# Liquid-scan block of a two-layer kernel: scan products per sequence, four array quadrants, stacked sums, full-row biases and a new order of all engines

## What is computed

```python
x = x + liquid_scan_block(attention_1(x))     # L0_cond, then L0_attn
x = x + experts(attention_2(x))               # L0_cond2, then L0_ffn

# the scan block, 512 channels d, 16 states n, one sequence at a time
xn = rmsnorm(x); x_in, z = split(xn @ in_proj_w); x_in = silu(x_in)
a_mod = sigmoid(x_in @ A_proj_w + A_proj_b)
B, C  = x_in @ B_proj_w, x_in @ C_proj_w
h_t = a_t[:, None] * sigmoid(A_base) * h_{t-1} + B_t[None, :] * x_t[:, None]
y_t = h_t @ C_t
out = x + ((y + D * x_in) * silu(z)) @ out_proj_w
```

## Time and profile before

| | us |
|---|---|
| median of 3 runs (lowest, highest) | 1818.32 (1817.47, 1819.48) |
| the profiled execution | 1821.07 |
| its span, first to last instruction | 1819.1 |
| PE busy in the span | 1633.8 (90%) |
| DVE, ACT, POOL busy | 1153.7 (63%), 915.6 (50%), 857.0 (47%) |
| one iteration in the steady stretch | 51.5 |

### The profile page before, as it was taken

One profiled execution on the slowest core, in us unless ns is written; L12 is line 12 of the kernel. 1 busy time (PEld: TensorE's weight loads), 2 busy tenths in 40 slices (PEclk: granted clock), 3 DMA queues, 4 the chain that ended last, 5 costly groups with the idle time before them and its releaser, 6 DMA issues.

```text
span 1819.1 us, 32943 instructions
## 1 busy us (share of the span) xinstructions
PE 1633.8 (90%) x11663; PEld 1264.5 (70%) x11663; DVE 1153.7 (63%) x2536; ACT 915.6 (50%) x2231; POOL 857.0 (47%) x552
## 2 busy tenths in 40 slices
PE   2248999999999999999999999999999999999875
PEld 1136777777777777777777777777777777777653
DVE  2465666677667666676676666776676666766533
ACT  0224555555555555565555555555555555655421
POOL 1024555554444555554445555544445555545431
PEclk9579999999999999999999999999999999999987
DMA  7110000000000000000000000000000000000000
GB/s 223 53 30 7 2 10 10 10 1 11 10 10 10 10 10 10 4 8 11 10 10 10 10 10 10 1 10 10 11 10 10 10 10 4 8 10 7 7 4 6
DMA packets 40357, 28.19 MB, mean 15 GB/s; under 512 B 19826, under 2 KB 38274, under 8 KB 40196
## 3 DMA queue, kind: packets, MB, share of 16 engines
q1 hardware_dynamic: 40196, 26.09, 5.5%
HBM read 21.37 MB, written 4.71 MB: 14 GB/s over the span
## 4 chain that ended last, share of the span: by engine, by line
PE 71%; ACT 10%; DVE 10%; issue 6%; SPq 2%; POOL 1%; DMA 0%; POOLq 0%; DVEq 0%; ACTq 0%
PE bank L736 13%; PE bank L674 13%; PE bank L702 7%; PE bank L813 6%; PE bank L628 5%; PE bank L630 5%; PE bank L629 5%; ACT a_prob L989 5%; PE bank L828 3%; PE bank L715 3%; PE bank L658 2%; DVE a_sum L1258 2%; DVE a_xn L1185 2%; PE bank L728 2%; SPq L454 2%
## 5 line engine op out<-in xcount | busy, mean ns | idle before, releaser
L1598 POOL TENSOR_TENSOR resid<-xres,a_c 128x256 f32<-128x256 f32 x32 | 23.2, 726 | 337.8 <-DVE x L1359 337.7
L1618 POOL TENSOR_TENSOR y<-y,u 128x512 f32<-128x512 f32 x128 | 162.9, 1272 | 39.1 <-DVE u L1351 34.0
L1610 POOL TENSOR_TENSOR u<-xe,Ef 128x512 f32<-128x512 f32 x96 | 130.2, 1370 | 35.1 <-ACT Ef L1086 35.1
L674 PEld LDWEIGHTS bank<-a_xnT,a_wq 128*128 128x128 f32 x1024 | 125.3, 193 | 17.2 <-issue 14.1
L813 PE MATMUL bank<-u,Gm 128*128 128x512 f32 x256 | 130.7, 614 | 4.5 <-DVE Gm L1343 3.8
L628 PE MATMUL bank<-w_e_hi,cT_hi 128*128 128x512 f32 x256 | 120.8, 472 | 10.2 <-DVE c_c L1407 10.2
L736 PEld LDWEIGHTS bank<-a_wo,a_prob 128*128 128x128 f32 x512 | 95.7, 192 | 48.9 <-ACT a_prob L989 36.9
L736 PE MATMUL bank<-a_wo,a_prob 128*128 128x256 f32 x512 | 119.6, 387 | 10.5 <-ACT a_prob L989 10.5
L674 PE MATMUL bank<-a_xnT,a_wq 128*128 128x128 f32 x1024 | 126.0, 277 | 0.0
L1579 POOL TENSOR_TENSOR a_prob<-a_prob,a_mask 128x1024 f32<-128x1024 f32 x32 | 75.6, 2361 | 104.9 <-DVE a_prob L1229 104.9
L674 PE MATMUL bank<-c_xnT,c_wq 128*128 128x128 f32 x1024 | 124.5, 280 | 0.0
(11 more groups left out here) (290 smaller groups left out, 4406.8 us busy)
## 6 DMA issues: line engine op xcount, KB each, us to landing
a_xin<-in_x SPq DMA_DIRECT2D x32, 128.0 KB, 2.6
xres<-in_x SPq DMA_DIRECT2D x32, 128.0 KB, 2.7
out<-acc SPq DMA_DIRECT2D x32, 128.0 KB, 1.7
a_wq<-in_L_cond_Wq SPq DMA_DIRECT2D x1, 1024.0 KB, 5.0
a_wo<-in_L_cond_Wo SPq DMA_DIRECT2D x1, 1024.0 KB, 6.3
c_wq<-in_L_cond_Wq SPq DMA_DIRECT2D x1, 1024.0 KB
c_wo<-in_L_cond_Wout SPq DMA_DIRECT2D x1, 1024.0 KB
u<-in_L_ffn_expert_w SPq DMA_DIRECT2D x3, 256.0 KB, 4.7
```

The costliest lines, as they stand in the source:

```text
L674: mm = pe.matmul(bank(f"q{half}")[:, m * P:(m + 1) * P], X.wq[:, k, hp * P:(hp + 1) * P], X.xnT[:, k, :], start=k == 0, stop=k == KD - 1)
L1610: pool.tensor_tensor(u[l][:, :], xi[:, :], (E0u if l == 0 else Ef[l])[:, :], ALU.mult)\
L1618: pool.tensor_tensor(y[:, :], y[:, :], tm[l][:, :], ALU.add).then_inc(g.done(f"y{l}"), 1)
```

## The change

Nothing of the result changes; the scan's pair products are confined to one sequence, where the mask had zeros before.

- **G** becomes two float32 matmuls, one for each sequence, of a 128 x 64 operand with 256 columns; `Gm`, the mask and the signs `sums` have 64 instead of 128 columns for each level.
- **mix** becomes two steps, `m0` (levels 0 and 1) and `m1` (levels 2 and 3). Each issues four products of 64 x 64 with 512 columns. The even level ("s", straight) writes each sequence to its own half of bank `m0s`, the odd level ("x", crossed) writes each sequence to the other half of bank `m0x`. So both row halves write into one bank. For the odd levels DVE's product with `Ef` is two instructions of 64 partitions.
- **E**: for each sequence `nl_stacked[b]` holds the high part in its own 64 partitions and the low part in the other 64. One fp32r matmul with the signs of two levels side by side (128 x 128) gives both levels of one sequence: 4 matmuls instead of 8. ACT then takes `exp` per level and sequence, 10 instructions of 64 partitions instead of 5 of 128; the high part takes two `Ln` of 64 partitions and a wait behind them, DVE's low part two instructions.
- **Biases**: decay bias, expert bias and their all-ones or one-hot operands get 128 rows (zeros elsewhere).
- **Order and banks**: `ORDER` and `TURNS` are written anew. Among others `a.W` (output projection of the first attention) and its statistics go from lag 1 to 2, so for tile 0 behind the second setup; SP issues the position-bias transfers one iteration earlier, ahead of iteration 3's loads.

```diff
-    pe.matmul(banks["b.G"][:, :], BTt[:, :], CD[:, :, :], start=True, stop=True)
+    for b in range(BT):
+        seq = slice(b * S, (b + 1) * S)
+        mm = pe.matmul(banks["b.G"][seq, 0:NLV * S], BTt[:, seq], CD[:, :, seq], start=True, stop=True)
...
-    for n, part in enumerate(nl_parts):
-        mm = pe.matmul(banks[f"b.E{l}"][:, :], sums[:, l * P:(l + 1) * P], part[:, :], start=n == 0, stop=n == 1)
+    pe.matmul(banks[f"b.E{n}"][:, :], sums[:, pair * P:(pair + 1) * P], nl_stacked[b][:, :], start=True, stop=True)
...
-    pe.wait_ge(*pool.at(f"u{l}", t))
-    pe.matmul(banks[f"b.m{l}"][:, :], Gm[:, l, :], u[l][:, :], start=True, stop=True)
+    for unit, l in (("s", straight), ("x", crossed)):
+        for b in range(BT):
+            seq, side = slice(b * S, (b + 1) * S), b if unit == "s" else 1 - b
+            mm = pe.matmul(banks[f"b.m{pair}{unit}"][side * S:(side + 1) * S, :],
+                           Gm[seq, l, :], u[l][seq, :], start=True, stop=True)
...
+    for i in range(2):
+        l = 2 * pair + i
+        src = banks[f"b.E{n}"][i * S:(i + 1) * S, :]
+        if l == 0:
+            act.activation(E0u[seq, :], src, ACT.Exp).then_inc(a.done(f"E0u{b}"), 1)
...
+        act.activation(Ef[l][seq, :], src, ACT.Exp, scale=-1.0).then_inc(a.done(f"E{l}{b}"), 1)
...
-    a_bias_parts = sb("decay_bias", [33, 2, D + NST], F32R)
+    a_bias_parts = sb("decay_bias", [P, 2, D + NST], F32R)
...
-    b_e_parts = sb("b_e_parts", [LVW + NE, D], F32R)
+    b_e_parts = sb("b_e_parts", [P, D], F32R)
...
 TURNS = {
+    2: """
+        b.E3@3>act.E31 b.m0s@3>dve.t0 b.xt@2>dve.yl b.x@2>dve.xi c.xt@3>act.xnT c.S1@3>dve.S1""",
...
+    6: """
+        c.ex3@5>dve.ac7 b.m1x@3>dve.t3 b.z@2>dve.zi b.E0@2>act.E10""",
+    7: """
+        b.E1@3>act.E11 b.m0x@3>dve.t1 c.W@4>dve.cn c.q0@3>act.q0 c.S0@3>dve.S0 c.oT@4>act.oT b.G@2>dve.Gm""",
```

More of the change, by code:

```diff
@@ L90, in constants @@
     parts["neg_count_c"] = -np.stack(count_c, 1)
-    parts["scan_mask"] = np.concatenate(masks, 1)
+    parts["scan_mask"] = np.concatenate([np.tile(a[0:S, 0:S], (2, 1)) for a in masks], 1)
     parts["level_rows"] = (tok[:, None] // LVW == np.arange(NLV)[None, :]) * 1.0
@@ L95, in constants @@
     parts["distance"] = (S - 1 - tok)[:, None]
-    parts["sums"] = np.concatenate(sums, 1)
+    stacked = [np.tile(a[0:S, 0:S], (2, 1)) for a in sums]
+    parts["sums"] = np.concatenate(stacked, 1)
     at, n = {}, 0
@@ L107 @@
     "pe": """
[L108 to L111, removed]
+        b.E1@3 c.ex2@5 b.E3@3 a.W@2 c.ex3@5 b.m0@3 c.eb@5 a.xt@1 c.PT0@4 c.PT1@4 a.kv@1 c.O@4 b.m1@3 a.q0@1
@@ L119 @@
[L119 to L122, removed]
+        b.BC@3 c.qs@4 c.ac1@5 a.mk@1 b.ag@3 c.S0@4 c.S1@4 b.nh@3 a.st@0 b.zi@3 b.Gm@3 c.ac2@5 c.mx@4 c.sub@4
+        c.ac3@5 c.ac4@5 c.den@4 a.st2@2 c.ac5@5 c.ac6@5 a.c@2 c.ac7@5 c.out@5 b.t0@3 b.t1@3 b.xn@2 b.t2@3
@@ L123 @@
+        b.t3@3 a.K@1 a.V@1 b.yl@2 c.st2@4 c.c@4 a.xn@0 c.cl@4 a.S0@1 b.xg@2 c.lg@4 c.oh@4 c.ac0@4 c.mk@3
+        b.xi@2 b.x1@3 c.st@3 c.xn@3 a.S1@1 c.ks@3 b.xl@2 a.mx@1 c.V@3 a.sub@1 c.K@3 b.zg@2 a.den@1""",
     "pool": """
[L124 to L125 removed]
+        a.norm@2 c.addb@4 c.addm@4 b.dx@3 b.u0@3 b.u1@3 c.norm@4 b.u2@3 b.u3@3 b.y0@3 b.y1@3 b.y2@3 b.y3@3
+        b.y@3 a.addm@1 c.qsq@3 b.resid@2""",
@@ L126 @@
     "sp": """
[L127 removed]
+        a.mask@1 b.xres@3 a.x@0 c.mask@3 c.store@5""",
 }
@@ L370, in build @@
         nl = yT[:, :, :].rearrange("p k n -> p (k n)")
-        nl_parts = parts("nl", [P, E2])
+        nl_stacked = [sb(f"nl_seq{b}", [P, E2], F32R) for b in range(BT)]
         ae = nl
@@ new lines, in G, with E @@
+                    mm.then_inc(p.done("G"), 1)
+                def E(n):
+                    pair, b = n // BT, n % BT
+                    def run(t):
+                        pe.wait_ge(*banks.free(f"b.E{n}", t))
+                        if n == 0:
+                            pe.wait_ge(*dve.at("nl1", t))
+                        pe.matmul(banks[f"b.E{n}"][:, :], sums[:, pair * P:(pair + 1) * P], nl_stacked[b][:, :],
+                                  start=True, stop=True).then_inc(p.done(f"E{n}"), 1)
@@ L833, in scan @@
                         "G": G, "yT": yT_, "out": out_} | {f"E{l}": E(l) for l in range(NLV)}\
-                    | {f"m{l}": mix(l) for l in range(NLV)}
+                    | {f"m{n}": mix(n) for n in range(NLV // 2)}
             def experts():
@@ L1063, in log_a @@
                     act.wait_ge(*p.at("E3", t - 1))
-                    act.activation(nl_parts[0][:, :], ae[:, :], ACT.Ln).then_inc(a.done("nh"), 1)
+                    for b in range(BT):
+                        seq = slice(b * S, (b + 1) * S)
+                        act.activation(nl_stacked[b][seq, :], ae[seq, :], ACT.Ln).then_inc(a.done(f"nh{b}"), 1)
+                    act.wait_ge(*a.at("nh1", t))
                     act.activation(nl[:, :], ae[:, :], ACT.Ln).then_inc(a.done("nl"), 1)
@@ L1113, in oT @@
                     act.wait_ge(*p.at("eb", t - 1))
-                    act.copy(ohT[:, :], banks["c.oT"][0:LVW + NE, 0:P]).then_inc(a.done("oT"), 1)
+                    act.copy(ohT[:, :], banks["c.oT"][:, 0:P]).then_inc(a.done("oT"), 1)
                 return {"cT": cT_, "le": le_, "oT": oT}
@@ L1328, in nh @@
                     dve.wait_ge(*p.at("E3", t - 1))
-                    dve.tensor_tensor(nl_parts[1][:, :], nl[:, :], nl_parts[0][:, :].bitcast(F32), ALU.subtract)\
-                       .then_inc(d.done("nl"), 1)
+                    for b in range(BT):
+                        seq, other = slice(b * S, (b + 1) * S), slice((1 - b) * S, (2 - b) * S)
+                        dve.tensor_tensor(nl_stacked[b][other, :], nl[seq, :], nl_stacked[b][seq, :].bitcast(F32),
+                                          ALU.subtract).then_inc(d.done(f"nl{b}"), 1)
                 def BC(t):
```

128 lines of the change are left out of this document (63 added, 65 removed), and 5 rows, old and new, of the table RESULTS.

## The result

The changed kernel takes 1857.0 us (median of 4 runs, 1848.0 to 1862.5) beside 1818.9 for the kernel before on the same chip: the ratio is 1.0197, its 95% interval 1.0146 to 1.0247. It is slower by about 2%, and 142 us above the forecast of 1715. The profiled execution took 1854.69 us, its span 1852.9; 30 intervals of an iteration make up nearly all of it, so I read one iteration first, from one E0 to the next. Columns as in the earlier trace rows: busy us and instructions of PE, PE's weight loads, DVE, ACT and POOL, then the clock.

What follows compares the result with a forecast made beforehand. PE was taken as the bound: 46.5 us of work plus a 1.9 wait gave a 48.4 us iteration, 3.1 shorter. 30 x 3.1 + 7 + 3 = 103 us saved gave 1715 us, range 1665 to 1788.

Steps and rivals of the forecast that it cites:

- PE's work, 46.5 an iteration: PE's busy time per iteration falls from 49.94 to 46.5 us through mixes, G, E and biases, less a loss for order.
- Rivals 1 and 2: In new mixes, row halves take turns at a bank (about 1788, 0.10), or quadrants do not overlap (about 1854, 0.05).
- the expert bias: On PE, the expert-bias product falls from 0.31 to about 0.12 us as a full product; gain 0.39 with its successor.
- The half instructions: DVE's two instructions for the low part of `nl`, taken at 0.7 to 1.43 us each.
- the first path: From c's last score product through ACT's exponentials, `prob`, `den` and `norm` to c.PT0: about 15.0 us.
- the second: From `nl` through DVE's low-part halves, statistics and `zi` to E0, then PE's work up to c.PT0: 13.2 to 14.7 us.
- The stall of 1.9 ahead of c.PT0: PE waits 1.9 us per iteration for the softmax's `norm` ahead of c.PT0, or in parts at earlier waits.
- The query-norm wait of 1.3 goes.: PE's 1.3 us wait for the second attention's query norms disappears, because a score step now stands between `qs` and `qt`.
- Rival 3: Longer softmax path, from slower ACT halves and DVE's contention with POOL or a late bank: 1748 to 1781 us, chance 0.18.
- The clock: PE ran at full clock (2.4 GHz, granted 1.00) before; the forecast has no term for a lower one.
- The ends, 7 + 3: Outside the steady iterations: 7 us gained at the start by an earlier second setup, 3 us in the draining.

Runs made afterwards that it cites:

- nl in PSUM: Changed kernel in the same order, but ACT writes the exact logarithm to a free PSUM bank, so DVE's low-part halves read PSUM and SBUF: 1769.0 us, ratio 0.9691 to before.

## Why the prediction was wrong, step by step

- *PE's work, 46.5 an iteration.* Right: 46.3 in the changed kernel, 46.49 with nl in PSUM. Rivals 1 and 2 (row halves in turn, no overlap) are out: a group of mixes costs what PV costs. Only the expert bias missed its price, 0.32 for 0.12, behind the small form.
- *The half instructions, "0.7 to 1.43 each".* This is the step that failed. They took 2.42 each. The upper end was read from the earlier trace rows as a price, and it was a price beside one particular neighbour, POOL's y product of 1.31 us. POOL's row of the kernel before shows it:

```profile
949.55 1.31 POOL L1603 TENSOR_TENSOR y<-xe,d_row 128x512 f32<-128x512 f32 x1
```

  POOL ends at 950.86, the low part at 951.40, 0.54 later. In the new order the neighbours are `addb` and `addm`, 2.4 each: read as "until POOL is done, then 0.55" the two halves come to about 5 us, and E0 to about 8 after the scores instead of "4.3 to 5.8" (measured 8.4, 967.49 to 975.90). The order of the instructions, which was known, told who the neighbours would be. The Trainium skill, SBUF — State Buffer (Who interferes with whom), says that a DVE instruction with two SBUF inputs contends with a GpSimd instruction that reads SBUF, and that the loser is blocked for the whole instruction. The trace agrees (0.55 behind POOL's end, three times), and nl in PSUM agrees with its counterpart, that a DVE instruction with at most one SBUF input, outside the 2-port performance modes, does not contend (0.70).
- *"An error in the first path alone gains little."* The two paths were weighed, and the second was taken to be just as long; with E0 at 8.4 and 8.9 of PE work behind it, it ends at 17.3 even at full clock, 2.3 behind the 15.0 of the first.
- *The stall of 1.9 ahead of c.PT0 or in parts before it.* As a mechanism right, and seen once the halves were cured: from the end of the scores to c.PT0 it is 15.65 us with nl in PSUM (974.95 to 990.60; forecast 15.0), with 1.4 of it waited ahead of `m0`. In the changed kernel it was hidden behind the longer wait.
- *"The query-norm wait of 1.3 goes."* 0.85 of it stayed, until `qs` was reached earlier on DVE. Its cause in the kernel before was not read; by these rows it is a wait of the same kind. There `qss`, for which PE waits 1.3, stands right behind a DVE instruction with a single SBUF tensor (`a_xn`), which runs beside POOL's normalization, ends 0.14 after it and takes 1.99, against 0.40 in the changed kernel:

```profile
947.63 1.96 POOL L1585 TENSOR_TENSOR a_prob<-a_prob,a_rden 128x1024 f32<-128x1024 f32 x1 [2.22 <-DVE a_rden L1263]
947.74 1.99 DVE L1185 TENSOR_SCALAR a_xn<-a_xin,a_mv,a_rstd 128x256 f32<-128x256 f32 x1
949.76 0.29 DVE L1219 TENSOR_SCALAR qss<-bank 128x128 f32<-128x128 f32 x1
```

- *Rival 3, the softmax path longer, with DVE's contention with POOL (0.18).* It named the cause, but priced it at about 1 us. Once the halves were cured the kernel lies in its band (1769 in 1748 to 1781, iteration 49.6); the exponentials, 0.61, lie between its 0.67 and my 0.53.
- *The clock.* The sum had it at 1.00. It cost 1.39 us an iteration behind a wait that the sum did not have; E0 was on the list of possible places, but with a wait of about 2.
- *The ends, 7 + 3.* The second setup did start earlier (58.7, forecast near 56), but W of tile 0 queues behind it for 11 us: 0.6 is left, and the drain is 1.5 longer.

In sum: 2.9 more idle time and 1.4 of clock, or 4.2 by the intervals of W (52.40 instead of 51.26 - 3.1), times 30 is 127; 11 at the ends; 138 of the 142 us. By the runs, the price of the halves alone is 88 of the 142 us (nl in PSUM). The rest is mainly 39 for an iteration still 1.3 longer than forecast (49.45 by the intervals of W), which holds the query-norm wait, and about 10 that the ends did not give.

## What to carry to other kernels

When an edit puts a DVE instruction with two SBUF inputs, or a TENSOR_SCALAR from SBUF to SBUF, at a new place, look up which POOL instructions will run beside it, and price it by their ends, not by its own duration elsewhere; or let one input of the two come from PSUM. When the busiest engine gets less work, the slack of every path beside it shrinks by as much: here 3.4 us were taken from PE, and each path with less slack than that came up in turn, and moving one step only passed the wait on. A wait of PE is to be priced with the clock that follows it.
